# Gathers that copy their own indices, target logits through PE, and a lighter gating of each fourth tile

## The reference, cut to what matters

```python
h = (x_flat @ W_gat).reshape(M, HEADS, NUM_EXPERTS)      # M = nodes, 4 heads x 4 experts
a_src = (h * att_src).sum(-1); a_dst = (h * att_dst).sum(-1)
e = leaky_relu(a_src[src] + a_dst[dst], 0.2)
ee = exp(e - segment_max(e, dst)[dst])
alpha = ee / (segment_sum(ee, dst)[dst] + 1e-16)
agg = segment_sum(h[src] * alpha[:, :, None], dst).reshape(M, 16) + b_gat
scores = layernorm(agg, ln_gamma, ln_beta).reshape(M, HEADS, NUM_EXPERTS).mean(1)
topk_s, topk_i = top_k(scores, 2); w = softmax(topk_s)
out = 0
for ei in range(4):                                      # every expert on every node
    g = where(topk_i == ei, w, 0).sum(-1)
    out += g[..., None] * (gelu(x @ W1[ei] + b1[ei]) @ W2[ei] + b2[ei])
```

## Time and profile before

| what | us |
|---|---|
| median of 3 runs | 1071.6 (1069.84 to 1073.52) |
| the profiled execution | 1072.75 |
| its span in the trace | 1071.0 |
| PE busy, share of the span | 793.4 (74%), mean granted clock 0.869 |
| DVE busy | 668.0 (62%) |
| ACT busy | 355.3 (33%) |
| POOL busy | 180.1 (17%) |

### The profile page before, as it was taken

One profiled execution on the slowest core, in us unless ns is written; L12 is line 12 of the kernel. 1 busy time (PEld: TensorE's weight loads), 2 busy tenths in 40 slices (PEclk: granted clock), 3 DMA queues, 4 the chain that ended last, 5 costly groups with the idle time before them and its releaser, 6 DMA issues.

```text
span 1071.0 us, 15105 instructions
## 1 busy us (share of the span) xinstructions
PE 793.4 (74%) x4837; PEld 519.7 (49%) x4837; DVE 668.0 (62%) x1393; ACT 355.3 (33%) x552; POOL 180.1 (17%) x179
## 2 busy tenths in 40 slices
PE   4369920017999989989988788799759877662688
PEld 1212220016887878878853233444327555442477
DVE  3599778755656656646648777595664434435764
ACT  3421130004544544545542333430022443333451
POOL 5180010000000000000022000100001366773021
PEclk9589965557999999999999899999977988886599
DMA  8000000001000000000000000000012200010001
GB/s 310 0 1 1 1 0 0 2 39 42 2 1 0 0 0 0 0 0 0 0 0 1 0 0 0 2 1 0 2 42 16 8 7 7 7 6 4 3 21 59
DMA packets 15645, 15.63 MB, mean 15 GB/s; under 512 B 9664, under 2 KB 13376, under 8 KB 15216
## 3 DMA queue, kind: packets, MB, share of 16 engines
q1 hardware_dynamic: 12544, 14.00, 4.3%
q0 software_dynamic: 3056, 1.08, 1.7%
HBM read 10.42 MB, written 4.65 MB: 14 GB/s over the span
## 4 chain that ended last, share of the span: by engine, by line
PE 19%; DVE 16%; issue 12%; POOL 3%; DMA 2%; DVEq 2%; ACT 2%; POOLq 0%; PEldq 0%; PEld 0%; SPq 0%; ACTq 0%
PE banks L1557 17%; DVE kept L1229 2%; POOL rows_g L592 2%; DMA rows_g<-table_d,g_idx 2%; DVE wide_buf L1189 1%; DVE wide_buf L1195 1%; PE banks L1838 1%; DVE tie L1193 1%; DVE kept L1292 1%; DVE kept L1386 1%; DVE T L867 1%; DVE round_k L1291 1%; PE banks L1590 1%; DVE shared L1384 1%; ACT wide_buf L776 1%
## 5 line engine op out<-in xcount | busy, mean ns | idle before, releaser
L1138 DVE TENSOR_TENSOR wide_buf<-banks,small 128x1024 f32<-128x1024 f32 x72 | 88.2, 1225 | 117.9 <-ACT small L726 117.9
L1557 PE MATMUL banks<-wide_buf 128*128 128x256 f32 (+1 forms) x720 | 144.6, 349 | 0.0
L1557 PEld LDWEIGHTS banks<-wide_buf 128*128 128x128 f32 x720 | 122.3, 194 | 12.6
L1557 PEld LDWEIGHTS banks<-XP 128*128 128x128 bf16 (+1 forms) x1552 | 101.8, 132 | 47.2 <-DVE XP L992 27.6
L1557 PE MATMUL banks<-XP 128*128 128x32 bf16 (+1 forms) x1552 | 102.4, 213 | 29.5 <-DVE XP L992 27.4
L592 POOL DMA_INDIRECT rows_g<-table_d,g_idx x88 | 95.5, 1085 | 132.2 <-issue 100.4
L1557 PE MATMUL banks<-taps_w,small 128*128 128x128 f32 x618 | 92.2, 296 | 21.0 <-issue 21.0
L1557 PE MATMUL banks<-T,XP 128*128 (+1 forms) x128 | 73.7, 701 | 38.2 <-ACT XP L789 33.3
L1557 PEld LDWEIGHTS banks<-taps_w,small 128*128 128x128 f32 x618 | 85.6, 203 | 31.7 <-issue 22.0
L724 ACT ACTIVATE small<-banks,neg_x 128x512 f32<-128x512 f32 x72 | 49.6, 690 | 150.1 <-PE banks L1557 124.2
L1557 PE MATMUL banks<-shared,sel 128*128 x216 | 60.2, 385 | 32.8 <-DVEq L1131 26.0
(11 more groups left out here) (330 smaller groups left out, 1190.9 us busy)
## 6 DMA issues: line engine op xcount, KB each, us to landing
wide_buf<-in_edges SPq DMA_DIRECT2D x2, 1536.0 KB, 15.4
generic_d<-generic SPq DMA_DIRECT2D x1, 2064.0 KB, 7.3
X<-in_x SPq DMA_DIRECT2D x4, 512.0 KB, 5.3
out_x<-X SPq DMA_DIRECT2D x4, 512.0 KB, 2.6
rows_g<-table_d,g_idx POOLq DMA_INDIRECT x88
wide_buf<-in_edges SPq DMA_DIRECT2D x2, 512.0 KB, 10.0
XP<-in_m_w SPq DMA_DIRECT2D x2, 512.0 KB, 4.7
taps_w<-in_w_dcn SPq DMA_DIRECT2D x1, 576.0 KB, 16.3
```

Source lines behind the costliest of these rows:

```text
L1138: nc.vector.tensor_tensor(near_w[s % RING], banks[:, 0:2, :], hat_x[:, h:h + 1, :].to_broadcast([P, 2, CHUNK]), ALU.mult).then_inc(w_done, 1)
L1557: return nc.tensor.matmul(o, l, r, start=start, stop=stop, **kw)
```

## The change

Three things, with what they need.

1. POOL copies the 4 indices of a half from `slot_idx` to `g_idx` itself, waits for its copy, and issues the 4 gathers. DVE no longer copies indices. Its one-hot pick of the target logits is split by halves and stands ahead of the wait for that half's rows.
2. `a_dst` goes to `bucket_dst` by 16 matmuls with the identity on PE and one DVE copy, without the two DMAs. For that the buckets are dealt out differently: partition p holds bucket `p % 32 * 4 + p // 32` (`neg_lo` is now an input, loaded by a POOL DMA). The first chunk's experts are written out on PE, with these 16 matmuls in it. `slot_ends` moves ahead of the wait for the last row. The order of output places in the slot sums follows the new buckets.
3. Of each chunk's four node tiles, the fourth is gated by ACT (one copy with a scale) and DVE (three multiply-adds), node by node, and PE turns the result with one matmul in place of four products. DVE waits for all expert outputs ahead of the first diagonals.

```diff
@@ POOL, set-up
-            for own, name in ((neg_y, "neg_y"), (neg_x, "neg_x"), (y_win, "y_win"), (x_own, "x_own")):
+            for own, name in ((neg_y, "neg_y"), (neg_x, "neg_x"), (neg_lo, "neg_lo"), (y_win, "y_win"), (x_own, "x_own")):
                 pool.dma_start(own[:, :], a[name]).then_inc(wa_in, 16)
...
-            nc.gpsimd.iota(neg_lo[:, :], [[0, 1]], base=0, channel_multiplier=-(1 << 17),
-                           allow_small_or_imprecise_dtypes=True).then_inc(made2, 1)
+            pool.sem_inc(made2, 1)
@@ SP
-            sp.wait_ge(adst_ready, 1)
-            sp.dma_start(table_d_dst.rearrange("(t p) h -> p t h", p=P), a_dst[:, :, :]).then_inc(adst_in, 16)
...
-            sp.wait_ge(adst_in, 16)
-            sp.dma_start(bucket_dst[:, :, :], table_d_dst.rearrange("(p t) h -> p t h", t=HIS)).then_inc(adst_in, 16)
@@ POOL, gather
                 for half in range(2):
-                    pool.wait_ge(idx1_ready, asked + half + 1)
+                    cols = slice(half * HALF_STEP, (half + 1) * HALF_STEP)
+                    pool.wait_ge(max1_done, g * 2 + half + 1)
                     pool.sem_inc(passed, 1)
-                    pool.wait_ge(max1_done, free + half + 1)
+                    nc.gpsimd.tensor_copy(g_idx[:, cols], slot_idx[:, bass.ds(r * STEP + half * HALF_STEP, HALF_STEP)]).then_inc(idx1_ready, 1)
+                    pool.wait_ge(idx1_ready, g * 2 + half + 1)
                     pool.sem_inc(passed, 1)
                     for k in range(HALF_STEP):
...
@@ ACT, gating
-                for e in range(EXPERTS):
-                    last = nc.scalar.activation(gate_diag[i % 2][:, 3, e, :], ident[:, :], ACT.Copy, scale=gate[:, 4 * i + 3, e:e + 1])
-                last.then_inc(diag_act, 1)
+                nc.scalar.activation(gate_diag[i % 2][:, 3, 0, :], y_exp[0][:, i, 3 * P:4 * P], ACT.Copy,
+                                     scale=gate[:, 4 * i + 3, 0:1]).then_inc(diag_act, 1)
@@ DVE, slot_step
+                for half in range(2):
+                    cols = bass.ds(r * STEP + half * HALF_STEP, HALF_STEP)
+                    grid = [P, HALF_STEP, HEADS, HIS]
+                    step(nc.vector.tensor_tensor(oh_slots, his[:, cols].unsqueeze(2).to_broadcast([P, HALF_STEP, HIS]),
+                                                 lane[:, 0:HIS].unsqueeze(1).to_broadcast([P, HALF_STEP, HIS]), ALU.is_equal))
+                    step(nc.vector.tensor_tensor(pick_grid, oh_slots.unsqueeze(2).to_broadcast(grid),
+                                                 bucket_dst[:, :, :].unsqueeze(1).to_broadcast(grid), ALU.mult))
+                    step(nc.vector.tensor_reduce(z_by_head[:, :, cols].rearrange("p h k -> p k h"), pick_grid, AX_X, ALU.add))
                     for landed in rows_landed[half]:
                         dve.wait_ge(landed, g * (16 * 2) + 16 * 2)
...
+                    nc.vector.tensor_copy(feat_s[:, :, cols], rows_step[:, half, :, 0:HE].rearrange("p k f -> p f k"))
                     step(nc.vector.tensor_tensor(z_by_head[:, :, cols], z_by_head[:, :, cols],
                                                  rows_step[:, half, :, HE:ROW].rearrange("p k h -> p h k"), ALU.add))
                     dve.sem_inc(max1_done, 1)
@@ DVE, ahead of the loop
             dve.sem_inc(max1_done, 2)
+            dve.wait_ge(dst_turned, 1)
+            run(nc.vector.tensor_copy(bucket_dst[:, :, :].rearrange("p h t -> p (h t)"), ps[6][:, 0:P]))
+            slot_ends()
...
-            slot_ends()
-            dve.wait_ge(adst_in, 32)
@@ DVE, gating
+                dve.wait_ge(diag_act, i + 1)
+                last_tile = gate_diag[i % 2][:, 3, 0, :]
+                for e in range(1, EXPERTS):
+                    step = nc.vector.scalar_tensor_tensor(last_tile, y_exp[e][:, i, 3 * P:4 * P], gate[:, 4 * i + 3, e:e + 1], last_tile,
+                                                          ALU.mult, ALU.add)
+                    if e + 1 < EXPERTS:
+                        run(step)
+                step.then_inc(diag_dve, 1)
...
+            dve.wait_ge(my_done, 2 + CHUNKS * EXPERTS)
             diagonals(0)
@@ PE, first chunk of the experts
-            with pe.Fori(0, CHUNKS - 1) as i:
+            hidden(0, 0)
+            hidden(0, 1)
+            expert_out(0, 0)
+            pe.wait_ge(adst_ready, 1)
+            for q in range(4):
+                part = slice(q * HIS, (q + 1) * HIS)
+                for h in range(HEADS):
+                    last = mm(ps[6][part, h * HIS:(h + 1) * HIS], a_dst[:, :, h], ident[:, part], True, True)
+            last.then_inc(dst_turned, 1)
+            hidden(0, 2)
...
+            with pe.Fori(1, CHUNKS - 1) as i:
                 experts(i)
@@ PE, slot_sums
                 for p in range(P):
-                    j, q = divmod(p, 4)
+                    q, j = divmod(p, HIS)
@@ PE, gating
-                pe.wait_ge(diag_dve, i + 1)
-                for j in range(CHUNK // P):
-                    if j == 3:
-                        pe.wait_ge(diag_act, i + 1)
+                pe.wait_ge(diag_dve, 2 * i + 1)
+                for j in range(3):
                     for e in range(EXPERTS):
...
+                pe.wait_ge(diag_dve, 2 * i + 2)
+                mm(out_[:, 3 * P:4 * P], gate_diag[i % 2][:, 3, 0, :], ident[:, :], False, False, skip_group_check=True).then_inc(gated, 1)
```

More of the change, by code:

```diff
@@ L327, in metaformer_kernel @@
         rows_landed = [[rows1_in, sem("rows1_b")], [sem("rows2_in"), sem("rows2_b")]]
-        adst_ready, adst_in, keys_there = (sem(n) for n in ("adst_ready", "adst_in", "keys_there"))
+        adst_ready, dst_turned, keys_there = (sem(n) for n in ("adst_ready", "dst_turned", "keys_there"))
         ends_ready, ends_turned, oh_ready, k_chain, s_chain = (sem(n) for n in (
@@ L581, in _, with gather @@
             pool.wait_ge(table_out, 16)
-            def gather(asked, free):
+            def gather(g, r):
                 for half in range(2):
-                    pool.wait_ge(idx1_ready, asked + half + 1)
+                    cols = slice(half * HALF_STEP, (half + 1) * HALF_STEP)
+                    pool.wait_ge(max1_done, g * 2 + half + 1)
                     pool.sem_inc(passed, 1)
-                    pool.wait_ge(max1_done, free + half + 1)
+                    nc.gpsimd.tensor_copy(g_idx[:, cols], slot_idx[:, bass.ds(r * STEP + half * HALF_STEP, HALF_STEP)]).then_inc(idx1_ready, 1)
+                    pool.wait_ge(idx1_ready, g * 2 + half + 1)
                     pool.sem_inc(passed, 1)
@@ L593, in gather @@
                                                 bass.IndirectOffsetOnAxis(ap=g_idx[:, c:c + 1], axis=0)).then_inc(rows_landed[half][k // 2], 16)
+            pool.wait_ge(ends_ready, 1)
             with pool.Fori(0, steps) as r:
-                gather(2 * r, 2 * r)
+                gather(r, r)
             with pool.If(rest > 0):
                 with pool.Fori(0, rest) as k:
+                    pool.wait_ge(ends_ready, k + 2)
+                    pool.sem_inc(passed, 1)
                     with pool.Fori(0, STEPS) as r:
-                        gather(k * (2 * STEPS + 2) + (2 * STEPS + 2) + 2 * r, k * (2 * STEPS) + 2 * STEPS + 2 * r)
+                        gather(k * STEPS + STEPS + r, r)
                     pool.nop()
@@ L1337, in slot_keys @@
                 step(nc.vector.tensor_tensor(slot_idx[:, 0:P], slot_idx[:, 0:P], slot_lo, ALU.add))
-                for half in range(2):
-                    halves = slice(half * HALF_STEP, (half + 1) * HALF_STEP)
-                    step(nc.vector.tensor_copy(g_idx[:, halves], slot_idx[:, halves]))
-                    dve.sem_inc(idx1_ready, 1)
                 step(nc.vector.tensor_scalar(slot_int, slot_int, 12, None, ALU.arith_shift_right))
@@ L1370, in rows_in @@
                         dve.sem_inc(passed, 1)
-                    step(nc.vector.tensor_copy(g_idx[:, half * HALF_STEP:(half + 1) * HALF_STEP], slot_idx[:, bass.ds(at + STEP, HALF_STEP)]))
-                    dve.sem_inc(idx1_ready, 1)
-                    step(nc.vector.tensor_copy(feat_s[:, :, bass.ds(at, HALF_STEP)], rows_step[:, half, :, 0:HE].rearrange("p k f -> p f k")))
-                def logits_in(half):
-                    cols = bass.ds(r * STEP + half * HALF_STEP, HALF_STEP)
+                    nc.vector.tensor_copy(feat_s[:, :, cols], rows_step[:, half, :, 0:HE].rearrange("p k f -> p f k"))
                     step(nc.vector.tensor_tensor(z_by_head[:, :, cols], z_by_head[:, :, cols],
@@ L1885, in _ @@
             pe.sem_inc(my_ready, 2)
-            with pe.Fori(0, CHUNKS - 1) as i:
+            hidden(0, 0)
[8 more added lines that the diff above has]
+            hidden(0, 2)
+            expert_out(0, 1)
+            hidden(0, 3)
+            expert_out(0, 2)
+            expert_out(0, 3)
+            with pe.Fori(1, CHUNKS - 1) as i:
                 experts(i)
```

28 lines of the change are left out of this document (8 added, 20 removed).

## The result

The changed kernel takes 1084.22 us (median of 4, 1079.48 to 1089.60), the kernel before 1071.07 beside it (4 runs, 1069.84 to 1073.52): a ratio of 1.0121, interval 1.0062 to 1.0181. It is slower, where I had forecast 1065.8. The profiled execution took 1080.96 at a span of 1079.2 and a mean granted clock of 0.868 (1.00 is full speed); the one of before that is compared with it has a span of 1071.0.

What follows compares the result with a forecast made beforehand. DVE's work behind each gather landing was taken to bound the loop, with ACT's expert stream close behind. Terms -10.4 + 8.7 - 4.1 = -5.8 gave 1066.9 us profiled, 1065.8 median; range 1057 to 1077.

Steps and rivals of the forecast that it cites:

- Who is late next: ACT: Expert copies ahead of the slot multiply: last late signal goes, one more wait possible; L1407 at 976.0, -10.4 us.
- Rival D: ACT's expert copies beside gathers: with POOL never pausing long, late signals could last a step; time 1078.2, chance 0.13.
- Start of the loop: Gather loop's start: less DVE work after the last row, second round of gathers at about 843.9, 6.4 us earlier.
- the cover of 0.9: Before the loop: DVE's wait for turned matmuls, copy and one-hot grid fit its 10.34 us idle, 0.9 us to spare.
- Period: Gather loop: DVE leaves the circle, POOL is the limit; half 6.15 us, step 12.3 instead of 12.91.
- The chain that I used for that distance: From DVE's last loop step to the slot multiply: L1407 follows 5.5 us behind, so 967.9 gives 973.4.
- Slot sums: PE's 256 slot-sum records serialise in one column group: 13.65 us at clock 0.50, before 4.98, +8.7.
- rival B: Slot sums don't serialise, or the clock rises: +0 to +2 instead of +8.7; time 1057 to 1060, chance 0.17.
- Gates: From the slot sums to the gates: DVE's 23 us move as a block, no change in time.
- Gating: Output gating: a chunk takes 3.87 us in place of 4.43, DVE setting the pace by a hair; -4.1 us.
- C: Gather loop: POOL's index copy costs near its upper bound, step 14.7 us, time 1086, mostly 1070 to 1077; chance 0.15.
- E: Gather loop gains nothing, POOL's copy giving back what DVE's shorter part wins; time 1076, chance 0.05.

Runs made afterwards that it cites:

- the gather part alone: Kernel before with only the first part of the change (POOL copies indices, DVE's one-hot grid by halves): 1062.73 us, ratio 0.9909.
- the other two together: Changed kernel with its first part undone, so DVE copies indices and does a whole step's one-hot grid in one piece: 1058.93 us, ratio 0.9907.
- spread sums and a pause: Changed kernel with slot sums to four column groups in turn, POOL waiting each step for the first half's rows: 1058.27 and 1057.84 us.
- the pause in six steps: Changed kernel with slot sums over four column groups, POOL waiting for landed rows in the first six steps only: 1053.97 us, ratio 0.9841.

## Why the prediction was wrong

**The step that failed** is in "Who is late next: ACT", under the start and period of the loop. It says: "As the gathers now end near 965, the last late one should go", and one more wait for the earlier start; from this I took L1407 at 976.0, -10.4. It priced the late signals by when gathers end and left out what ends each wait. The profile of before carried it: of its nine waits, of up to 7.9 us, two end in POOL's pause of 1.88, four inside the held gather just ahead of it, one 0.34 us after the last gather and two elsewhere. The change removes the pause of 1.88 and shortens the multiply that held a gather for 2.18 from 2.00 to 0.69, and single waits grow to 10.7 us in this profile (13.6 in others) and a pass from some 19 to 26 us to 43. That a pause or the longer multiply brings them down again is shown by the runs above; by which mechanism is not. In place of -10.4 the stretch came to +13.3, with the last copy at 992.62.

**Rival D** had place and mechanism right, and its point of decision (a last copy from 978.4 on) was passed by 14 us. Its sizes were off. It left one whole pass for the end of the gathers; there were two and a half. It put that end at 968 (the step above says 965), which was 954.80. I gave it 0.13, arguing that the waits "have two pauses a step now". The loop has two gaps of 0.98, but what before's waits had ended on were 1.88 and a held gather. Two shorter gaps did not replace one long one: of the ten waits in the changed kernel's profile two end in such a gap.

**What only the chip decides.** On the chip without late signals the kernel gained 22.8 us, far beyond my best case of 1057. There each term of the sum can be read without D:

- Start of the loop. Forecast: second round at 843.9. Measured 841.61 with an origin 0.9 earlier, so 1.4 better. The turned matmuls took 1.49 us for 32 records, 46.6 ns each; the 0.9 us that "PE has 0.9 more work" counts for them is shown by no run. On the measured chip DVE saw their signal late, at 826.45. That looks to be within the 829.5 that I had named, but counted from PE's turned ends it is 10.46 where my limit was 9.55 (8.62 without late signals): the cover of 0.9 did not hold, and DVE's work for the last row starts 16.46 behind that point and not 15.40. It cost nothing, as DVE later stood 32.76 us for ACT.
- Period. Forecast 12.3 (gap 1.25, hold 0.2); measured 11.5: gap 0.98 and holds of 0.1 (0.2 to 0.46 for three gathers near the end). I had halved the old multiply to 1.0 and overlooked that the second part's layout lets DVE read the logits in order: 0.69. Nine steps by 0.8 are 7 us.
- With both, DVE ends at 959.06 and not 967.9, and with ACT out of the way the multiply follows 5.5 later, at 964.57. The chain that I used for that distance was right, the 2.6 us that I added for ACT are not needed there.
- Slot sums. The serial order was right. The 53.3 ns of "256 x 53.3" no run shows; the runs showed 52.6 and then 44.4 ns a record at 0.50 and 26.7 at 1.00, so 53.3 was near for the first 2 us alone. "No gap added" held: PE was busy for 9.94 of the 10.00 us. "The clock was 0.50 in that stretch, ... so I keep 0.50" was wrong: measured +5.0 for +8.7. Of rival B one half, no serial order, is out: spread again, the stretch is back at 5.1 to 5.6. The other half, a rising clock, came true, but only some 5 us into the stretch, so that it cost +5.0 and not B's 0 to +2.
- Gates: -0.7 for 0, from ACT's exponential being ready sooner (DVE waits 0.43 in place of 1.04).
- Gating. Forecast 3.87 a chunk and -4.1; measured 3.76 and -5.3, alone in the old kernel -4.6 (0.9961). DVE keeps PE's pace, so my "by a hair" fell on the other side.
- Rivals C and E are out: the copy costs 0.98 in all, and the loop alone gains.

The three parts also do not add. On chips with late signals the gather part alone gave 7.7 us (one chip), and the other two together 10.2 (another); all three cost about 10 to 23 in the comparisons here. Missing in my sum was the product of two edits: POOL that never waits, by the first, and the shorter multiply, by the second. Undoing either brings the kernel below the one before (1058.93 and 1059.56).

The range, 1057 to 1077, thus missed on both sides, depending on the chip. From the profile of before it could not be read that the signals are late on some chips and not on others; that its 49 us of unexplained waits deserved more than 0.13, could.

A version that beats the kernel before on each chip where it ran is the changed kernel with spread sums and a pause: 1058.27 without late signals and 1057.84 with them; with the pause in six steps, on one chip with late signals, 1053.97. On the chip without late signals the changed kernel itself stays the fastest (1048.00).

## What to carry to other kernels

A wait that the profile gives to nobody is a cost with a cause: find what ends it before you remove the idle time that may be ending it. Here POOL's idle 1.88 us a step, off the critical path, helped to keep the path short. And when two edits touch the same loop, price them together: one made POOL dense, the other made DVE brief, and only kernels with both lost.

Where a result hangs on such waits, time the kernel on more than one chip. The kernel before differed by nothing that a median shows, and the same changed kernel came out at 0.979 and at 1.023.

## What the runs showed of the hardware

- PE's signals arrive late beside indirect gathers of POOL (remote waits of ACT's expert copies, 839 to 970 us, of 9.9 to 76.0 us a profile): at ACT in the two profiles of the first comparison and on three of the four chips of the experiments, with single waits of up to 13.6 us, and without gathers never (passes of 15.3 on one of the same chips). On one chip they are not late at all beside the same gathers. DVE's copy of the turned logits shows it too. In all eleven profiles with these 16 matmuls beside gathers on chips with late signals it waits 6.5 to 8.0 us (in the first, for matmuls that had ended some 2 us earlier); on the chip without late signals it waits 4.5 to 4.9, and without gathers 4.6. With a pause of about 2 us in the gathers a late signal mostly lands 0.9 to 1.7 us after the end of the gather ahead of it. Why chips differ stays open.
- A gather that POOL begins 0.07 us or more into DVE's multiply of the one-hot grid by the logits ends 0.80 to 0.85 us after the multiply does, or takes its usual 0.94 to 0.97 if that is longer. That makes 2.18 beside a multiply of 2.00, 1.40 beside 1.22, 1.41 to 1.48 beside 1.07 to 1.11 and 1.03 beside 0.69, and 1.40 beside 0.69 where the gather begins 0.11 into it. One that began 0.03 into it or earlier is hardly held: 0.94 to 1.06, three times 1.20 (857.79, 0.61 ahead of the multiply at 858.40, takes 0.95). So the hold depends on the phase as much as on the multiply.
- Beside gathers that multiply takes, for 512 elements, 0.69 us with both tensors read in order (once 0.74 or 0.75 near the end of the loop in five profiles) and 1.07 to 1.12 us with one read across.
- 256 small records into one column group after another take 52.6 ns each in the first 2 us and 44.4 in the next 2 at a granted clock of 0.50, and 26.7 at 1.00; the clock rose some 5 us into that stretch. In four groups in turn they take 14.7 ns at 0.50 (187 in 2.75 us), and the clock stayed at 0.50 for the 5 us that this order needs.
